# Line gates of five images inside the transforms, one image's taps ahead of a small product, turned output and gate logits in one product, fetches one add earlier

## What is computed

```python
x_h = gx.mean(axis=3, keepdims=True); x_w = gx.mean(axis=2, keepdims=True)
hw = jnp.einsum('oc,bcln->boln', w1, cat) + b1[None, :, None, None]    # cat: x_h, x_w
gated = gx * jax.nn.sigmoid(xh_g) * jax.nn.sigmoid(jnp.transpose(xw_g, (0, 1, 3, 2)))
x1 = group norm of gated, per channel;  x2 = w_pw * (3x3 depthwise of gx)
s1 = softmax(x1.mean());  s2 = softmax(x2.mean())
wts = jnp.einsum('bc,bchw->bhw', s1, x2) + jnp.einsum('bc,bchw->bhw', s2, x1)
z = gx * jax.nn.sigmoid(wts[:, None] + freq_feat)      # freq_feat: from |rfft2(gx)|
t = tokens(x + z);  xt = layernorm(t)
S = jax.nn.sigmoid(xt @ Wg);  G, I = jax.lax.top_k(S, 2)
h = gelu(xt @ W1[e] + b1[e]);  y = h @ W2[e] + b2[e];  out = t + sum of G * y
```

## Time and profile before

| | |
|---|---|
| median of 3 runs | 351.88 us (349.36, 351.88, 352.78) |
| profiled execution | 352.2 us, of which the span from the first to the last instruction 349.7 |
| busy in the span | PE 304.1 us (87%), DVE 248.4 (71%), ACT 182.0 (52%), POOL 155.8 (45%) |
| chain that ended last | PE 53%, DMA 20%, DVE 20%, issue 3% |
| granted TensorE clock | 0.955 of full speed on average |

### The profile page before, as it was taken

How to read it: one execution, slowest core, us unless ns; L and a number is a source line. 1 busy time by engine, 2 the same in 40 slices (tenths; PEclk the granted TensorE clock), 3 DMA queues, 4 the chain that set the end, 5 groups by cost and what they waited for, 6 DMA issues and landing times.

```text
span 349.7 us, 8670 instructions
## 1 busy us (share of the span) xinstructions
PE 304.1 (87%) x3052; PEld 228.3 (65%) x3052; DVE 248.4 (71%) x588; ACT 182.0 (52%) x506; POOL 155.8 (45%) x161
## 2 busy tenths in 40 slices
PE   0989999999930688999979999999999999999960
PEld 0768733457730376888858888888888888877730
DVE  3795389768799889979785888797855655656430
ACT  3355668434553437666664857667545353454310
POOL 7021096427531350554554363554654544545241
PEclk9999999999975699999989999999999999999995
DMA  7400000001186754496975887889454343344310
GB/s 221 157 1 2 1 0 3 0 30 61 62 276 218 152 171 150 117 208 171 230 173 119 218 174 211 219 179 241 88 88 78 66 78 77 59 66 69 53 17 2
DMA packets 36185, 39.41 MB, mean 113 GB/s; under 512 B 8400, under 2 KB 32816, under 8 KB 36144
## 3 DMA queue, kind: packets, MB, share of 16 engines
q1 hardware_dynamic: 29168, 29.56, 29.9%
q0 software_dynamic: 6976, 9.31, 15.4%
HBM read 29.74 MB, written 9.11 MB: 111 GB/s over the span
## 4 chain that ended last, share of the span: by engine, by line
PE 53%; DMA 20%; DVE 20%; issue 3%; POOL 1%; SPq 1%; ACT 0%; POOLq 0%; ACTq 0%
DMA out<-fb,idx 15%; PE ps L869 12%; PE ps L856 6%; PE ps L858 6%; PE ps L854 6%; PE ps L870 6%; PE ps L690 4%; DMA fb<-xn_rows,idx 3%; PE ps L719 2%; DMA xt<-x_tok 2%; PE ps L723 2%; PE ps L726 2%; PE ps L808 2%; PE ps L670 2%; DVE wt L1051 2%
## 5 line engine op out<-in xcount | busy, mean ns | idle before, releaser
L869 PE MATMUL ps<-wt,fb 128*128 x312 | 117.7, 381 | 0.0
L645 ACT ACTIVATE fb<-ps,b1t 128x128 f32<-128x128 f32 (+7 forms) x312 | 81.9, 375 | 68.7 <-issue 59.2
L854 PE MATMUL ps<-fb,wt 128*128 128x128 f16 (+7 forms) x624 | 114.8, 215 | 2.6 <-DVE fb L1264 2.6
L856 PE MATMUL ps<-fb,wt 128*128 128x128 f16 (+7 forms) x624 | 114.9, 215 | 0.0
L858 PE MATMUL ps<-fb,wt 128*128 128x128 f16 (+7 forms) x624 | 114.8, 215 | 0.0
L514 POOL DMA_INDIRECT out<-fb,idx x39 | 64.4, 1651 | 104.3 <-DMA out<-fb,idx 71.1
L870 PE MATMUL ps<-wt,fb 128*128 x312 | 85.4, 274 | 0.0
L854 PEld LDWEIGHTS ps<-fb,wt 128*128 x624 | 61.2, 98 | 33.3 <-issue 3.9
L856 PEld LDWEIGHTS ps<-fb,wt 128*128 x624 | 60.7, 98 | 3.5
L858 PEld LDWEIGHTS ps<-fb,wt 128*128 x624 | 60.7, 98 | 0.0
L504 POOL DMA_INDIRECT fb<-xn_rows,idx x39 | 43.9, 1125 | 24.4 <-DVE idx L1242 12.8
(11 more groups left out here) (205 smaller groups left out, 383.3 us busy)
## 6 DMA issues: line engine op xcount, KB each, us to landing
wt<-w SPq DMA_DIRECT2D x32, 512.0 KB, 6.3
b2t<-b SPq DMA_DIRECT2D x39, 128.0 KB, 3.7
xt<-x_tok SPq DMA_DIRECT2D x4, 512.0 KB, 7.8
out<-xt SPq DMA_DIRECT2D x8, 256.0 KB, 2.1
xn_rows<-wt SPq DMA_DIRECT2D x8, 256.0 KB, 3.3
b1t<-params SPq DMA_DIRECT2D x39, 4.0 KB, 2.3
fb<-xn_rows,idx POOLq DMA_INDIRECT x39, 3.4
out<-fb,idx POOLq DMA_INDIRECT x39, 4.5
```

Of the source, the lines that this page charges most:

```text
L645: a = nc.scalar.activation(hid[:, s, f * P:f * P + ROWS[n]], h_ps(s)[:, f * P:f * P + ROWS[n]], ACT.Gelu_apprx_tanh, bias=b1t[:, n % NBIAS ...
L854: pe.matmul(dst, hi, xT[:, s, c * P:c * P + rows], start=(c == 0 and f % 4 == 0), stop=False, skip_group_check=True)
L856: pe.matmul(dst, hi, xT[:, s, (2 + c) * P:(2 + c) * P + rows], start=False, stop=False, skip_group_check=True)
L869: pe.matmul(y_ps(s), hhi[:, s, f * P:(f + 1) * P], w, start=(f == 0), stop=False)
```

## The change

The five edits:

1. `gate_lines` makes the line gates of tiles 0 to 9 (`EARLY_GATES`) in a product of 320 columns after image 5's transforms, and of tiles 10 to 15 in one of 192 columns at the old place; `gate_sigmoids` follows on ScalarE at the same places. GpSimd's row products of the first tiles can start then. VectorE takes six of its column gates and five statistics (`gate_rows`, three gates at a time) ahead of the square sums of the last two images. VectorE now has 13 of the 16 column gates instead of 12.
2. `taps(1)` stands ahead of the dwm product. It writes the bank that held the logits of x, so it waits for VectorE to have read them (`xlg_read`).
3. In `back` one product of 136 columns takes the place of a transpose and a product: z times the identity beside `wgc` (`turner`, which GpSimd fills). There are four per image, into two banks; VectorE sums the 8-column pieces of both halves per image (`z_logits`, into `zlg`) and reads the turned part where it stands.
4. The prefix sums of the tables go to bank 2.
5. In GpSimd's loop the fetch stands ahead of the add.

```diff
-DVE_GATES = 12
+EARLY_GATES = 10
+GATES_AT_ONCE = 3
+DVE_GATES = 13
...
+        turner = place(1, 0, 2 * HALVES * (P + E)).bitcast(F32).rearrange("p (a n) -> p a n", a=HALVES)
+        wgc = turner[:, :, P:P + E]
+        zlg = place(1, 2 * HALVES * (P + E), 2 * NBLK * E).bitcast(F32).rearrange("p (k e) -> p k e", e=E)
...
-                pool.wait_ge(gate_sig, t // CG + 1)
+                pool.wait_ge(gate_sig, 1 if t < EARLY_GATES else 2)
                 if t == 0:
                     pool.wait_ge(padded, POOL_PADS)
+                if t == 2 * POOL_PADS:
...
+                if i + LEAD < TILES:
+                    gather(i + LEAD)
                 if i >= LEAD:
                     add(i - LEAD)
-                if i + LEAD < TILES:
-                    gather(i + LEAD)
...
+            def gate_sigmoids(g, tiles):
+
+                act.wait_ge(gate_mm, g + 1)
+                lines = ps[:, 4, tiles.start * (H + W):tiles.stop * (H + W)].rearrange("p (t n) -> p t n", n=H + W)
+                nc.scalar.activation(sg[:, tiles, :], lines, ACT.Sigmoid, bias=col("b1"), scale=1.0 / H)\
+                    .then_inc(gate_sig, 1)
...
+                if b == EARLY_GATES // 2:
+                    gate_sigmoids(0, slice(0, EARLY_GATES))
...
+            def gate_lines(tiles):
+
+                pe.wait_ge(sq_done, tiles.stop)
+                if tiles.start > 0:
+                    pe.wait_ge(gate_sig, 1)
+                pe.matmul(ps[:, 4, tiles.start * (H + W):tiles.stop * (H + W)], w1d[:, :],
+                          rc[:, tiles, :].rearrange("p t n -> p (t n)"), start=True, stop=True).then_inc(gate_mm, 1)
...
+                if b == EARLY_GATES // 2:
+                    gate_lines(slice(0, EARLY_GATES))
                 if b > 0:
                     x_logits(b - 1)
             x_logits(B - 1)
-
-            pe.wait_ge(sq_done, NT)
-            pe.matmul(ps[:, 4, :], w1d[:, :], rc[:, :, :].rearrange("p t n -> p (t n)"),
-                      start=True, stop=True).then_inc(gate_mm, 1)
+            gate_lines(slice(EARLY_GATES, NT))
...
             taps(0)
+            pe.wait_ge(xlg_read, 1)
+            taps(1)
             pe.wait_ge(small_ready, 3)
             pe.matmul(ps[0:NT, 5, 128:256], dwm[:, :], wpwd[:, :], start=True, stop=False)
             pe.matmul(ps[0:NT, 5, 128:256], ones_row[0:1, 0:NT],
                       par[0:1, PAR["bpwrow"]], start=False, stop=True).then_inc(small_mm, 1)
-            for u in range(1, 4):
+            for u in range(2, 4):
...
                 for k in range(2):
                     for a in range(HALVES):
-                        m = pe.transpose(ps[:, BACK[b % 2], (2 * k + a) * P:(2 * k + a + 1) * P],
-                                         z[:, 2 * b + a, k * P:(k + 1) * P], ident)
+                        m = pe.matmul(ps[:, BACK[b % 2] + k, a * (P + E):(a + 1) * (P + E)],
+                                      z[:, 2 * b + a, k * P:(k + 1) * P], turner[:, a, :], start=(a == 0),
+                                      stop=(a == HALVES - 1), skip_group_check=True)
                 m.then_inc(zt_done, 1)
-                for k in range(2):
-                    o = (2 * b + k) * E
-                    for a in range(HALVES):
-                        m = pe.matmul(ps[:, 4, o:o + E], z[:, 2 * b + a, k * P:(k + 1) * P], wgc[:, a, :],
-                                      start=(b == 0 and k == 0 and a == 0), stop=(a == HALVES - 1), skip_group_check=True)
...
+            def gate_rows(first, end):
+
+                for t in range(first, end):
+                    if t < DVE_GATES:
+                        gate(t)
+                    if t > 0:
+                        gate_stats(t - 1)
+
             for b in (B - 2, B - 1):
+                gate_rows(GATES_AT_ONCE * (b - B + 2), GATES_AT_ONCE * (b - B + 3))
                 power(2 * b)
                 power(2 * b + 1)
...
+            gate_rows(2 * GATES_AT_ONCE, EARLY_GATES + 2)
+            dve.wait_ge(exp_done, 2)
+            link(v.tensor_reduce(out=s2s[:, 1, :], in_=row(1), axis=AX_X, op=ALU.add))
+            link(v.reciprocal(s2s[:, 0, :], s2s[:, 1, :]))
+            v.tensor_tensor(out=row(2), in0=row(1), in1=wide(0), op=ALU.mult).then_inc(small_ready, 1)
+            gate_rows(EARLY_GATES + 2, NT)
+            link(gate_stats(NT - 1))
...
+            def z_logits(b):
+
+                dve.wait_ge(zt_done, b + 1)
+                return v.tensor_reduce(out=zlg[:, 2 * b:2 * b + 2, :], axis=AX_X, op=ALU.add,
+                                       in_=turned(b)[:, :, :, P:P + E].rearrange("p k a e -> p k e a"))
+
             def add_x(b):
-                dve.wait_ge(zt_done, b + 1)
-                v.tensor_tensor(out=xt[:, 2 * b:2 * b + 2, :], in0=ps[:, BACK[b % 2], :].rearrange("p (k c) -> p k c", c=C),
-                                in1=xt[:, 2 * b:2 * b + 2, :], op=ALU.add).then_inc(t_done, 1)
+                t = xt[:, 2 * b:2 * b + 2, :].rearrange("p k (a n) -> p k a n", a=HALVES)
+                v.tensor_tensor(out=t, in0=turned(b)[:, :, :, 0:P], in1=t, op=ALU.add).then_inc(t_done, 1)
...
+                    z_logits(b - 2)
                     add_x(b - 2)
                     stats_t(b - 2)
 
 
-            dve.wait_ge(logit_mm, 1)
-            link(v.tensor_tensor(out=lg[:, :, :], in0=ps[:, 4, 0:NBLK * E].rearrange("p (k e) -> p k e", e=E),
-                                 in1=xlg[:, :, :], op=ALU.add))
+            link(z_logits(B - 1))
+            link(v.tensor_tensor(out=lg[:, :, :], in0=zlg[:, :, :], in1=xlg[:, :, :], op=ALU.add))
```

More of the change, by code:

```diff
@@ L444, in _ @@
             g = nc.gpsimd
+            pool.wait_ge(const_in, 48)
+            g.tensor_copy(turner[:, :, 0:P], cc("ident").unsqueeze(1).broadcast_to([P, HALVES, P])).then_inc(turner_set, 1)
             pool.wait_ge(pad_zero, 2)
@@ L573, in shift @@
                 a.then_inc(shift_done, 1)
-            act.wait_ge(gate_mm, 1)
-            for g in range(2):
-                n = NT // 2
-                nc.scalar.activation(sg[:, g * n:(g + 1) * n, :],
-                                     ps[:, 4, g * 256:(g + 1) * 256].rearrange("p (t n) -> p t n", t=n),
-                                     ACT.Sigmoid, bias=col("b1"), scale=1.0 / H).then_inc(gate_sig, 1)
+            gate_sigmoids(1, slice(EARLY_GATES, NT))
             shift(0)
@@ L1045, in _ @@
             v.tensor_scalar(dwm[:, :], dwm[:, :], 1.0 / PX, col("bdw"), ALU.mult, ALU.add).then_inc(small_ready, 1)
-            def gate(t):
-                dve.wait_ge(gate_row, t + 1)
-                gv = gated[:, t].rearrange("p (h w) -> p h w", w=W)
-                v.tensor_tensor(out=gv, in0=gv, in1=sg[:, t, H:H + W].unsqueeze(1).broadcast_to([P, H, W]),
-                                op=ALU.mult).then_inc(gated_done, 1)
             dve.wait_ge(small_mm, 2)
@@ L1060, in _ @@
             v.tensor_tensor(out=row(0), in0=logits, in1=wide(0), op=ALU.subtract).then_inc(exp_in, 1)
-            for t in range(NT):
-                if t < DVE_GATES:
-                    gate(t)
-                if t > 0:
-                    if t <= DVE_GATES:
-                        dve.wait_ge(gated_done, t)
-                    else:
-                        dve.wait_ge(gate_col, t - DVE_GATES)
-                    v.bn_stats(gbn6[:, t - 1, :], gated[:, t - 1, :])
-                if t == NT // 2:
-                    dve.wait_ge(exp_done, 2)
-                    link(v.tensor_reduce(out=s2s[:, 1, :], in_=row(1), axis=AX_X, op=ALU.add))
-                    link(v.reciprocal(s2s[:, 0, :], s2s[:, 1, :]))
-                    v.tensor_tensor(out=row(2), in0=row(1), in1=wide(0), op=ALU.mult).then_inc(small_ready, 1)
-            dve.wait_ge(gate_col, NT - DVE_GATES)
-            link(v.bn_stats(gbn6[:, NT - 1, :], gated[:, NT - 1, :]))
+            gate_rows(2 * GATES_AT_ONCE, EARLY_GATES + 2)
[5 more added lines that the diff above has]
+            link(gate_stats(NT - 1))
             for t in range(NT):
@@ L1177, in _ @@
             last, key_last, full_slots, nth_last, behind, moved, at_last, nth = [part[:, i, :] for i in range(8)]
-            counts = ps[:, 5, NBLK * E:(NBLK + 1) * E]
-            before = ps[:, 5, 0:NBLK * E].rearrange("p (k e) -> p k e", e=E)
+            counts = ps[:, 2, NBLK * E:(NBLK + 1) * E]
+            before = ps[:, 2, 0:NBLK * E].rearrange("p (k e) -> p k e", e=E)
             by_j = lambda x: x.unsqueeze(1).broadcast_to([P, E, E])
```

26 lines of the change are left out of this document (19 added, 7 removed).

## The result

The changed kernel takes 347.74 us in the median (346.96 to 349.64, six runs), the kernel before 351.36 in the runs beside it; the ratio is 0.9893 with a 95% interval of 0.9854 to 0.9933, 3.8 us less. Run again later (e5) it took 347.63. The prediction was 347.3. The runs of the kernel before lie far apart (348.65 to 364.15 in 29 of them), and the ratios here leave out those over 1.5% above the lowest of their kernel, while the medians count all.

A forecast was written before the change was run, and what follows sets the result against it. TensorE bounds transforms, maps and expert part (but for a late-fetch hole), nearly ties with VectorE in the middle; VectorE alone carries the chain after 94 us. 352.2 - 0.7 - 1.4 + 0.6 - 3.4 = 347.3 us; range 345.0 to 350.6.

The forecast's parts named there:

- case forecast: Whole kernel: the predicted terms hold, 345.6 to 348.9 us by its bounds; chance 0.62.
- Line gates and VectorE's gates: Transforms and middle: 0.56 us of product moves into the transforms and leaves the middle; gain nothing.
- in time, by 0.3: End of transforms: VectorE is through its early gates near 41.7 us, before the logits come at 42.0.
- Taps of image 1: Middle: taps ahead of dwm cut TensorE's waits from 1.79 to about 1.0 us; gain 0.7, ends 0 and 1.8.
- 4.2 us after the logits: Middle: when the dwm input is ready, 45.62 - 41.44 from the kernel before, so at 46.2 us.
- the first wait: Middle: first of TensorE's three waits for VectorE, 0.67 us; claimed to be hidden by the taps.
- VectorE's idle stretch: Middle: VectorE stands idle because TensorE gets to the dwm product 2.1 us later than before.
- Turned z and gate products: Maps: a `back` takes 0.95 us, 0.28 saved; five of eight stand before the last map, gain 1.4 us.
- the dearer price of 1.36: Maps: a `back` at the pace of L731's products would take 1.36 us, a loss of 0.13 each.
- The tail: Behind the last map: two VectorE reductions and a third with its hand-over lie on the chain; loss 0.6 us.
- Fetch ahead of add: Expert part: each fetch goes one add earlier, closing the hole near 180 us; gain 3.4 us, ends 0 and 3.9.
- The rival that the adds take the fetch's place: Expert part: late adds delay halves once, 3.9 us back, 350.7; one hole left or made again, chance 0.15.

The follow-up runs named there:

- e5: The changed kernel run once more, unaltered; 347.63 us, ratio 0.9844 to the kernel before.
- e4: The changed kernel with GpSimd's last six row gates held until VectorE has made the dwm input; 348.21 us, ratio 0.9891 to the kernel before.
- e10: The changed kernel with the dwm product ahead of the taps of image 1 again; middle 28.29 us, against 22.92 in the changed kernel.
- e12: The kernel before with every fetch one add later (behind add k the fetch of tile k+5); 390.94 us against 355.51.
- e7: The kernel before run once more, unaltered, for its profile; 22 adds took 122.82 us, the first add 23.91.
- e2: The kernel before with only line gates in two parts, VectorE's early gates and taps of image 1 ahead of the dwm product; ratio 0.9953.
- e3: The kernel before with only the turned z and gate products in one, their logits summed on VectorE; ratio 0.9972.
- e6: The changed kernel with the add ahead of the fetch again; 351.08 us against 347.63 for the changed kernel on the same chip.
- e1: The kernel before with only the fetch put ahead of the add; 350.34 us against 353.37, ratio 0.9946.
- e9: The changed kernel with GpSimd's last six row gates held, softmax two gates earlier, and SyncE issuing weights ahead of biases; 346.96 us, ratio 0.9798.
- e11: The changed kernel with row gates held and softmax two gates earlier, the dwm product ahead of image 1's taps again; middle 22.07 us against 21.57.

## Why the prediction came out right, and which of its steps did not

The time was right, 347.3 forecast and 347.7 measured, and the fetch pays, as the case forecast says. But two of its terms were mis-sized in opposite directions, and a third came out by another mechanism. That the figure fits to 0.4 us is in part luck: the sum took 4.9 us from 352.2, the one profiled execution, and the runs show 3.8 (by the ratio) from a median of 351.36, 0.8 lower.

*Line gates and VectorE's gates.* Right for TensorE: 0.50 us moved into the transforms (0.56 forecast), and nothing waits there. The row gates start where forecast (35.33 in e4, 35.3 forecast), but VectorE is not through with its six gates "in time, by 0.3": in all nine profiles with the early gates it reads the logits 0.67 us after they are there, and that is part of TensorE's wait for dwm. The early gates have a second price there that the step did not see, below.

*Taps of image 1.* 0.7 forecast, 0.6 measured, by the wrong wait. The step that failed is the one that took "4.2 us after the logits" from the kernel before for the time of dwm. It holds only while GpSimd starts half-way through that chain; with GpSimd at work all the time it is 5.90 to dwm's last step instead of 3.89 (e4: 2.74 without GpSimd). So dwm took the place of the first wait, and VectorE's idle stretch, 2.1 forecast, was only 0.80, which made s2r punctual. Without the taps ahead the gates make the middle 4.3 us longer than before (e10), of which 2.6 are the half clock behind the wait: the gates need the taps. Whether the taps gain anything without the gates no run shows.

*Turned z and gate products.* 0.95 us a turn forecast, 0.93 measured; the dearer price of 1.36, L731's, is out. The mis-sized term is the period: 5 x 0.40 = 2.0 gained instead of 1.4, since 1.25 us left (82.18 to 83.43 in the starts, where the chain's parts made 1.23) and the map's first product passes 0.08 faster behind a long product than behind eight short ones. The tail lost 0.38 instead of 0.6. Together 1.64 instead of 0.8, in every profile. The Trainium skill, page "TensorE: Matmul & The Clock Gate", section "Back-to-back issue gap", has loads and matmuls set the pace together; these rows do not show it for 136 columns, whose eight instructions take 0.116 us each, as the tap rate alone gives (136 x 0.89/512 / 2 halves = 0.118).

*Fetch ahead of add.* 3.4 us forecast, the term that was taken from one execution. The mechanism is right: TensorE waits for no fetch in the eight profiles with the fetch first, and one add later costs 35 us (e12). The size is not shown: in the profiles the expert part takes 223.3 us on average with the old order (five: before, e7, e2, e3, e6) and 222.8 with the new (eight), 0.5 apart and less than the spread; by timed runs it is 1.9 (e1) and 2.6 (e6 against e5), with 3.4 inside the interval of e1. The wait of 2.06 us was the longest of five: the others with the old order had 0.89 and 0.26 (e7), 0.28 (e2) and none (e3, e6). Why the timed runs show more than the profiles is open. They also lie closer together with the fetch first: 346.11 to 349.61 in e5 against 346.32 to 353.10 in e6, 349.24 to 353.76 in e1 against 348.65 to 364.15 in the kernel before on that chip; what the longest executions waited for no kept profile shows. The rival that the adds take the fetch's place is not what the changed kernel shows: behind 145 us TensorE waited for late halves in five of the eight profiles with the fetch first (0.6 to 1.5 us at a time), but in two of the five with the add first too (1.12 in e3, 0.25 in e6), and in the changed kernel behind weights that had landed late, not behind an add. Its mechanism is real, though: in e9, where no weights are late, both holes stand behind an add, with 0.58 and 0.90 us instead of 3.9.

The sum: 0.6 + 1.64 + 1.9 = 4.1 us, beside 3.8 by the ratio of the whole change. The ratios of the three parts agree with it: 0.9946 x 0.9953 x 0.9972 = 0.987, within the intervals of 0.9893 and 0.9844.

## What to carry to other kernels

Cut the profile at fixed instructions and look at which pieces repeat in a second profile: a piece that repeats to 0.02 us can carry a term, while a hole in a stretch full of transfers belongs to one execution until a second one has it. A duration of a small VectorE step holds only for the neighbours it ran with; when an edit moves GpSimd's work, take the steps' durations from rows where GpSimd was at work beside them. And weigh a queue's order by its slack, the lead in tiles times the time of a tile against the loop from add to fetch to add: here TensorE waited for no fetch with six tiles (eight profiles), for none, one or two with five (five profiles), and for 23 with four (e12).

## What was not expected of the hardware

Beside GpSimd's products some of VectorE's small steps take about three times as long, as shown above (0.18 to 0.60 us for 16 numbers, a copy of 48 from 0.20 to 0.55), and its reduction does not (0.30 in both). The Trainium skill, page "SBUF — State Buffer", section "Who interferes with whom", says that VectorE's instructions with two inputs in SBUF contend with a GpSimd instruction that reads SBUF, that copies can under conditions, and that a reduction never does on this chip; the rows agree, though a few of the two-input steps kept their 0.2 us.

TensorE's clock fell at 20 us in four of the fourteen profiles (before again, changed, e1, e11: 0.66 granted from 20 to 25 us, 1.00 in the others), and the transforms took 1.6 us longer then (30.92 in e7 against 29.33 in the kernel before; 31.76 in e1, which has other waits besides). Ahead of it stands a wait of about 1.1 us for VectorE with the clock kept (1.08 in the kernel before, 1.16 in e3) and lost (1.17 in the changed kernel). What decides is open.

The first tile's products stopped for "issue" (waits for nothing that the profile shows) between 124 and 133 us in twelve of the fourteen profiles, and in these the first add came 23.9 to 24.2 us behind the first fetch. The other two, the first one of the kernel before and e12, have no such stop, and 22.1 and 22.8. What was short there is not shown; the transfers were busy at 0.87 from 126 to 128 us in the changed kernel and at 0.63 in the kernel before.
